# A four-layer convolution block on one core: changes to the last stage (roots, output products, output stores, filler products)

## The reference

```
xc  = xq - mean                                  # per component and group
cov = einsum('cqn,cpn->cqp', xc, xc) / N         # a 4x4 matrix for each of the 16 groups
A   = cov + EPS * eye(4)
U   = cholesky(A).T
z   = solve_triangular(U, xc, lower=False)
out = einsum('pqc,qbchw->pbchw', weight, z) + bias
```

## Time and profile before

| | |
|---|---|
| median of 3 runs | 67.28 us (67.15 to 68.71) |
| the profiled execution | 67.17 us, of which its span (first to last instruction) is 65.4 us |
| PE busy | 56.9 us, 87% |
| DVE busy | 46.2 us, 71% |
| ACT busy | 42.5 us, 65% |
| POOL busy | 21.8 us, 33% |
| chain that ended last | PE 33%, DVE 5%, ACT 2%, issue 1% |

### The profile page before, as it was taken

The page is one execution under the profiler, slowest core; times in us unless marked ns, Lnnn a source line. Parts: engine busy times, 40 slices in busy tenths (PEclk is TensorE's granted clock), DMA queues, the critical chain, the costliest instruction groups (busy, mean ns, idle before and its releaser), DMA issues. The chain is left out here.

```text
span 65.4 us, 2158 instructions
## 1 busy us (share of the span) xinstructions
PE 56.9 (87%) x811; PEld 35.6 (54%) x811; DVE 46.2 (71%) x120; ACT 42.5 (65%) x138; POOL 21.8 (33%) x64
## 2 busy tenths in 40 slices
PE   5987898889999998995989898999899999999900
PEld 2332443557465635542436385599658998854500
DVE  0079899596757989996693856998478978576520
ACT  0710198999999499969999495680049445268620
POOL 5000863730373705775032108318212050054000
PEclk9999999999999999999999999999999999999999
DMA  0887970000000000000000000000000000000053
GB/s 0 234 242 133 318 319 13 0 0 10 0 0 0 5 0 0 0 10 10 0 0 0 0 10 0 0 0 10 0 0 0 10 0 10 0 0 0 0 193 128
DMA packets 2457, 2.71 MB, mean 41 GB/s; under 512 B 400, under 2 KB 2064, under 8 KB 2448
## 3 DMA queue, kind: packets, MB, share of 16 engines
q1 hardware_dynamic: 2160, 2.39, 11.8%
q10 hardware_dynamic: 288, 0.20, 1.0%
HBM read 2.06 MB, written 0.52 MB: 39 GB/s over the span
## 5 line engine op out<-in xcount | busy, mean ns | idle before, releaser
L711 PE MATMUL bank<-const-bfloat16-1.0 128*64 128x512 bf16 x64 | 9.2, 429 | 0.8 <-PEq L1379 0.8
L552 ACT ACTIVATE probs<-bank 128x512 f32<-128x512 f32 x16 | 8.8, 603 | 1.1 <-PE bank L794 1.1
L532 ACT ACTIVATE bank<-bank,negmax 128x256 f32<-128x256 f32 x20 | 9.1, 461 | 0.2 <-DVE negmax L1085 0.2
L833 PE MATMUL both<-probs,vt 128*64 128x256 f32 x56 | 7.6, 387 | 0.3 <-DVE cut L1095 0.3
L1085 DVE TENSOR_REDUCE negmax<-bank 128x2 f32<-128x512 f32 x10 | 6.7, 685 | 1.4 <-PE bank L770 0.8
L366 POOL TENSOR_TENSOR cut<-cut 64x256 f32<-64x256 f32 x7 | 4.3, 611 | 8.3 <-DVE cut L1095 5.3
L532 ACT ACTIVATE both<-both,negmax 128x256 f32<-128x256 f32 x12 | 5.4, 452 | 1.5 <-DVE negmax L1085 1.5
L941 PE MATMUL bank<-hi,taps 64*64 64x225 f16 (+2 forms) x126 | 5.9, 267 | 0.1
L941 PE MATMUL bank<-lo,taps 64*64 64x225 f16 (+2 forms) x126 | 5.9, 265 | 0.0
L711 PEld LDWEIGHTS bank<-const-bfloat16-1.0 128*64 128x64 bf16 x64 | 3.7, 119 | 3.7 <-issue 1.6
L941 PEld LDWEIGHTS bank<-hi,taps 64*64 64x64 bf16 x126 | 5.0, 107 | 0.6 <-issue 0.4
(11 more groups left out here) (154 smaller groups left out, 122.7 us busy)
## 6 DMA issues: line engine op xcount, KB each, us to landing
cw<-conv_w SPq DMA_DIRECT2D x2, 288.0 KB, 4.7
x<-x_in SPq DMA_DIRECT2D x4, 128.0 KB, 2.9
out<-res SPq DMA_DIRECT2D x4, 128.0 KB, 1.9
kst<-consts SPq DMA_DIRECT2D x1, 428.0 KB, 5.4
aw<-attn_w ACTq DMA_DIRECT2D x1, 128.0 KB, 2.7
aw<-attn_w SPq DMA_DIRECT2D x1, 128.0 KB, 4.0
half<-select SPq DMA_DIRECT2D x1, 96.0 KB, 2.7
kst<-consts SPq DMA_DIRECT2D x1, 64.5 KB, 4.0
```

What stands on the lines that cost most here:

```text
L532: nc.scalar.activation(part, part, ACT.Exp, bias=negmax[:, i % 2, n:n + 1], accum_out=total[:, i % 2, n:n + 1]).then_inc(total_out, 1)
L552: nc.scalar.activation(probs[:, i % 2, g], pb_t[g][:].rearrange("p (t n) -> p t n", t=CH), ACT.Exp).then_inc(exp_out, 1)
L711: mm(bank[lanes(h)], filler[:, lanes(h)], filled, start=True, stop=True)
L833: last = mm(mixed(i)[g * C:(g + 1) * C], vt[:, i % 2, t, g * C:(g + 1) * C], probs[:, i % 2, g, t, :], start=(t == 0 and i < ITERS - 1), s ...
```

## The change

Four edits, all in the last stage:

1. Root 1 moves from GpSimd to ScalarE, as `Ln` and `Exp` of the second pivot. GpSimd computes root 0, multiplies `hot` by it into `hot01[0]` (which ScalarE did before), and goes on to root 2, for which it waits for the second `pivot_out`. ScalarE makes `hot01[1]` from its own root 1 and GpSimd's `hot01[0]`.
2. Piece 3 of the output products writes to banks 1 and 3 instead of 6 and 7; the wait for piece 0's results goes away.
3. SyncE issues three stores; the fourth is issued by ScalarE, after its last result, once all results of ScalarE and VectorE are there.
4. The last number of `WARM` is 13 instead of 15.

```diff
-WARM = (4, 6, 2, 4, 1, 15)
+WARM = (4, 6, 2, 4, 1, 13)
-        pb_out = [[banks[n] for n in ns] for ns in ((6, 7), (4, 5), (2, 0), (6, 7))]
+        pb_out = [[banks[n] for n in ns] for ns in ((6, 7), (4, 5), (2, 0), (1, 3))]
@@ sync
-            for n in range(len(PIECES)):
+            for n in range(len(PIECES) - 1):
@@ gpsimd
-                pool.wait_ge(root_out, j + 1)
+                pool.wait_ge(root_out, 1 if j == 0 else 2)
             power(0)
-            for j in range(1, Q - 1):
-                pool.wait_ge(pivot_out, j)
-                power(j)
+            nc.gpsimd.tensor_scalar(hot01[0][:], hot, roots[:, 0:1], 1.0, ALU.mult, ALU.mult).then_inc(hot_pool, 1)
+            pool.wait_ge(hot_pool, 1)
+            pool.wait_ge(pivot_out, 2)
+            power(2)
@@ scalar
-            for n in range(2):
-                act.wait_ge(root_out, n + 1)
-                if n:
-                    act.wait_ge(hot_out, 1)
-                nc.scalar.activation(hot01[n][:], hot01[0][:] if n else hot, ACT.Identity,
-                                     scale=roots[:, n:n + 1]).then_inc(hot_out, 1)
+            act.wait_ge(pivot_out, 1)
+            nc.scalar.activation(lnp1[:], tt[:, 1, 1:2], ACT.Ln).then_inc(lnp1_out, 1)
+            act.wait_ge(lnp1_out, 1)
+            nc.scalar.activation(roots[:, 1:2], lnp1[:], ACT.Exp,
+                                 scale=kst[:, K_EXPO + 1:K_EXPO + 2]).then_inc(root1_out, 1)
+            act.wait_ge(root1_out, 1)
+            act.wait_ge(hot_pool, 1)
+            nc.scalar.activation(hot01[1][:], hot01[0][:], ACT.Identity, scale=roots[:, 1:2]).then_inc(hot_out, 1)
             act.wait_ge(pivot_out, Q - 1)
             ...
+            act.wait_ge(res_act, len(PIECES))
+            act.wait_ge(res_dve, len(PIECES))
+            act.dma_start(out[:, quarter(3)], res[:, quarter(3)]).then_inc(stored, 16)
@@ tensor
-                if n == 3:
-                    pe.wait_ge(res_act, 1)
-                    pe.wait_ge(res_dve, 1)
@@ vector
-            dve.wait_ge(hot_out, 2)
-            dve.wait_ge(root_out, Q - 1)
+            dve.wait_ge(hot_out, 1)
+            dve.wait_ge(root_out, 2)
```

More of the change, by code:

```diff
@@ L188, in build @@
         roots = sb("roots", [P, Q - 1])
-        lnp = sb("lnp", [P, 1])
+        lnp, lnp1 = sb("lnp", [P, 1]), sb("lnp1", [P, 1])
         hot01 = [sb(f"hot01{n}", [P, Q]) for n in range(2)]
@@ L265, in build @@
         pivot_out, root_out, piv_out, a_out = sem("pivot_out"), sem("root_out"), sem("piv_out"), sem("a_out")
-        lnp_out = sem("lnp_out")
-        hot_out = sem("hot_out")
+        lnp_out, lnp1_out, root1_out = sem("lnp_out"), sem("lnp1_out"), sem("root1_out")
+        hot_out, hot_pool = sem("hot_out"), sem("hot_pool")
         fw_out, fin_mm, stored = sem("fw_out"), sem("fin_mm"), sem("stored")
```

## The result

The changed kernel took 66.89 us (median of 7 runs); run beside the kernel before again in two later sets (2 and 4 of the table below), 66.73 (7 runs) and 66.68 (6). The ratio to the kernel before is 0.9926 [0.9897, 0.9954] in the first set, 0.9905 [0.9869, 0.9941] and 0.9902 [0.9874, 0.9930] in the later ones. With 67.2 us before, that is 0.50 to 0.66 us faster, 0.7 to 1.0%. Executions of either kernel fall in two groups some 1.4 us apart that differ only ahead of the changed stage, so the ratios are those of the lower group (the median of before in the first set, 68.71 us, lies in the upper one) and positions are counted from the start of `tt`, from where the two groups agree within 0.01 us.

A forecast was written before the change was run, and what follows sets the result against it. The kernel was taken to be bound by a single file of fillers, output products, VectorE's results and stores; 0.28 us (earlier products) plus 0.17 (last store) off 67.17 gave 66.72, forecast 66.7, range 66.3 to 67.1 for 8 in 10.

The forecast's parts named there:

- The hand-over from VectorE to TensorE: Delay from the end of VectorE's result to TensorE going on, read ahead of piece 3 as 0.12 us.
- The near tie at 60.75: At the start of the output products, the filler turns were said to hold them, only 0.05 us beyond `final_w`.
- Roots: Root 2 on GpSimd was to start at 58.90, 0.23 us earlier, moving `prod` to 59.59 and `final_w`'s end to 60.35.
- Cover on ScalarE: ScalarE's `hot01[1]` was to be done 0.49 us before `prod` starts; `piv` and `zc` had covers of 0.24 and 0.3.
- Fillers: Two fewer turns were to free TensorE at 60.30; `final_w`, ready at 60.47, then starts the output products 0.28 us earlier.
- Banks: Piece 3 follows piece 2 at once; VectorE's fourth result ends 0.25 us earlier, which alone would give nothing.
- Fourth store: Issued by ScalarE, last issue 0.77 us earlier; DMA engines serving stores one after another, 0.39 us each, leave 0.17 us gain.
- Free overlap: Rival for the stores at the end: they overlap freely, the last issue counts, 0.77 us gain, 66.40 us; chance 0.16.
- VectorE blocked by GpSimd: Rival: GpSimd's new product shuts out VectorE's elimination step, second pivot 0.19 us later, time 66.91 us; chance 0.10.
- Late store: Rival: the store from ScalarE's queue lands late, 2.7 us giving 67.16 and 4.0 us giving 68.46; chance 0.12.
- Signs: Expected in the profile after: 0.1 to 0.2 us gap before output products, last two landings 0.2 to 0.4 longer, DMA share near 1.
- Chances: For the kernel's time: 0.96 same within 2%, 0.02 faster than 65.94 us, 0.02 slower than 68.6 us.

## Why the prediction was right or wrong

The forecast was 66.7 us, 0.45 us under the profiled execution. The stage became 0.62 us shorter and the kernel 0.50 to 0.66 us faster, so sign and mechanism held and the sum was a quarter too small. Two of its terms were mis-sized. The hand-over from VectorE to TensorE, taken as 0.12 us, is 0.06; so the products start 0.35 us sooner and not 0.28. And the last store, with the banks, gave 0.21 us where the sum had 0.17. A further 0.06 is in no term of the sum: the last landing follows the last packet sooner. What sped that up is open, so this part of the gain is luck.

As a level, 66.7 stands against a median of three runs, 67.28, that was treated as firm. Beside the changed kernel, seven runs of the kernel before had their median at 68.71; held against that, 66.89 is a step of 1.82 us, three times what the stage became shorter. The change explains 0.62 of it, and the prediction had no term for the rest, though one of the three runs that it saw took 68.71.

The hand-over could have been read in the trace of the kernel before. Earlier in the same stage TensorE loads weights that wait for VectorE's `cov_q` alone:

```profile
56.81 0.17 DVE L1278 TENSOR_TENSOR cov_q<-cov,kst 128x16 f32<-128x16 f32 x1
57.04 0.30 PEld L1030 LDWEIGHTS both<-cov_q,kst 128*128 128x128 f32 x2 [0.23 <-DVE cov_q L1278]
```

The load follows the end of `cov_q` (56.98) by 0.06 us. With that the prediction's own sum gives 60.35 + 0.06 = 60.41 for the products, 0.34 us sooner.

Point by point:

- *The near tie at 60.75*: right in kind, wrong in size. The fillers held the products, by 0.11 us and not by 0.05. The failed term is the hand-over, which I took as 0.12 from the wait ahead of piece 3; it is 0.06 wherever `final_w` binds (60.44 to 60.50 here, 60.84 to 60.90 with the old roots). The 0.12 row was a wait for two engines' results; whether that is why it is longer was not tried.
- *Roots*: root 2 came 0.23 us sooner, as worked out, and `prod` 0.24. But the way there was not as put. GpSimd's product took 0.29 us instead of 0.20 and started 0.10 instead of 0.08 after root 0; it ended at 58.91, and with 0.08 us root 2 could start at 58.99. It started at 59.00, which is also 0.16 after the second pivot (58.84). The two waits came out equal; which one held it was not tried. The bound of 0.37 for the product covered this.
- *Cover on ScalarE*: `hot01[1]` is done at 59.31, 0.37 us before `prod`, instead of 0.49, and `piv` (59.94) 0.22 before `final_w` starts. Both covers held.
- *Fillers*: two turns fewer, and the products wait for `final_w`, 0.06 us after it. Fillers and roots are worth 0.11 and nothing alone, 0.35 together, as the argument of the tie said. The granted clock stayed at 1.00.
- *Banks*: right. VectorE's results follow each other without a gap (the last ends at 4.54 against 5.15). Alone that gives nothing at the end, as the prediction had it; with the fourth store on its own queue it is worth 0.10 us.
- *Fourth store*: right mechanism, small in size. Of 0.62 us, 0.35 belong to the products and 0.06 to the landing behind the last packet, which the sum put at nothing without a reason; stores and banks gave 0.21 where I had 0.17. The packets in the traces show where the term was short. From the first store's first packet to the last store's end it took 2.00 us before and 1.78 after, where I had 1.80 and 1.63. A store that I took as served in 0.39 us, as if it kept all engines busy, took some 0.5 from its first packet to its end: alone it does not fill them (shares of 0.69 to 0.87 between stores). That falls on both kernels. The difference is in when the last store's data begin: 1.23 us after the first's in the changed kernel, as worked out (1.24), but 1.48 before instead of 1.41. So the kernel before lost more between its stores than I counted. The Trainium skill says (DMA: Bandwidth & Descriptors, Issuing engines are not separate DMA queues) that transfers of different issuers interleave on the same 16 DMA engines and that a second issuer saves only issue time. The trace agrees: the last issue came 0.49 us sooner with the second queue, the engines were busy from 62.90 to 63.80 without a break, and the end came 0.21 us sooner.
- *Free overlap*: refuted (0.21 and 0.11 us, not 0.49 and 0.38). *VectorE blocked by GpSimd*: not put to the test. The new product started 0.01 us behind VectorE's elimination step (58.62 and 58.61), not ahead of it as the rival needs; the step took 0.23 us, as in the earlier trace rows. *Late store*: refuted, ScalarE's store landed after 1.8 us, and after 2.1 at most in the other kernels.
- *Signs*: the gap of 0.1 to 0.2 us between fillers and products does not show in the chain (60.49 to 60.50), because the modelled end of the last filler covers it. Of the last two landings only SyncE's grew, to 2.1 us; ScalarE's stayed at 1.8. The DMA share did rise to 1.
- *Chances*: by the ratio the time lies within 2% of before, as given 0.96, and 66.89 is in the range.

## What to carry to other kernels

Where a filler or another cheap cover ends within 0.1 us of the wait it covers, both have to be shortened together; each done alone shows next to nothing (0.11 us and none here, 0.35 together), and the bracket of the wait names only one of them. Take a hand-over's price from a wait of the same kind (one releaser, same engines), not from the nearest in time. At the end of a kernel, count what the last transfers cost the DMA engines: here a second issuing queue brought the last issue forward by 0.49 us and the end by 0.21.

## What the runs showed of the hardware

Two queues can issue at once: ScalarE's issue at 62.26 (0.35 us) and SyncE's at 62.40 (0.40) overlap, and neither is longer than alone (0.35 to 0.40 in the earlier trace rows). The Trainium skill (Perfetto Trace Analysis, DMA Instruction — HWDGE (DVE, Sync)) says that the block that makes descriptors is locked for one issuer at a time; no waiting of that kind shows here.

TensorE's first weight load came 0.06 us after the end of the VectorE instruction that it waited for alone (`cov_q` before, `final_w` in the changed kernel and with the old roots), and 0.12 us after the later of two engines' results (61.65 to 61.77 before).

The 16 increments by which a store reports its landing came 12 ns apart in three kernels and 7 ns in all others, 0.06 us at the end of the kernel; they go with the buffer and the semaphores declared (see under the table), not with the roots, the banks, the fillers or the queue.

A store of 64 KB costs the DMA engines 0.23 us and one of 128 KB 0.40, and lands 1.6 to 1.7 us after issue instead of 1.7 to 2.1.

GpSimd's product of four columns took 0.29 us where it started 0.01 us after VectorE's elimination step, against 0.20 for a two-input operation of its size and 0.37 for a `TENSOR_SCALAR` of one column elsewhere. Whether the step held it up was not tried.
